# Third layer of a hyperbolic convolution: the sum over tokens as eight accumulated matmuls and a mask

## The chip, the cores and the metric

The kernel runs on one core of a Trainium2 chip. The metric is the device time of one execution in microseconds (us), as the median of several runs. TensorE (PE), VectorE (DVE), ScalarE (ACT) and GpSimd (POOL) run side by side and meet at semaphores; SyncE (SP) issues most transfers. All data are float32.

## The reference, cut to what matters

Eight stages work on x, which has 8 x 32 x 32 tokens of 64 channels, and each adds its result to x: a cosine transform, an expert layer, a dense convolution, an expert layer, the hyperbolic convolution that is changed here, an expert layer, a spherical transform, an expert layer. The hyperbolic one has three layers, each a fully connected map in the ball followed by a batch norm in the ball. The batch norm begins with a midpoint over all tokens:

```python
def midpoint(x):
    lx = lam(x)                       # 2 / (1 - |x|^2), one number for a token
    m = jnp.sum(lx * x, 0) / jnp.clip(jnp.sum(lx - 1.0, 0), TINY)
    n = jnp.sqrt(jnp.clip(jnp.sum(m * m), TINY))
    m = jnp.tanh(0.5 * jnp.arctanh(jnp.minimum(SC * n, ATANH_CLIP))) * m / (SC * n)
    return project(m)

def hbatchnorm(x, bias_pt, weight):
    mu = midpoint(flat)
    var = jnp.mean(dist(flat, mu) ** 2)
    v = logmap(mu, flat)
    v = transp(mu, bias_pt, v)
    v = jnp.sqrt(weight / (var + BN_EPS)) * v
    return expmap(bias_pt, v).reshape(shp)
...
out = hrelu(hbatchnorm(hconv(x, z1, 1, 1, 0, 64), bn1_bias, bn1_weight))
out = hrelu(hbatchnorm(hconv(out, z2, 3, 1, 1, 16), bn2_bias, bn2_weight))
out = hbatchnorm(hconv(out, z3, 1, 1, 0, 16), bn3_bias, bn3_weight)
out = hrelu(project(mobius_add(out, x)))
```

What matters is the numerator of the midpoint: a sum over all 8192 tokens of a number for the token times its row of channels, and, next to it, the sum of lam - 1 and every token's product with the bias.

## The kernel before

**Tiling.** The 8192 tokens lie on 128 partitions and in 64 tiles: X[p, t, c] holds channel c of token (p, t). A number for each token is a [128, 64] array (k.scalars), the values of the first two layers are V16 with 16 channels, those of the third V64 with 64, so that one DVE instruction on the third layer's values has 4096 elements on each partition. W1 and W2 are work arrays of the same shape.

**Stages.** `program` runs the eight stages one after the other; each is a block of its own with a barrier of all engines behind it. `hyper_stage` is the fifth.

**Order inside the stage.** The function `hyper` is written once and run by DVE, ACT and PE, each of which issues only its own steps. `Turns.step` counts the steps of each engine and lets an engine wait for a given count of another; `Ball.dve` makes every DVE step wait for the DVE step before it too. So DVE's order is the order of the text, and what is late there is late for all behind it. PE and ACT wait only for what a step names.

**The batch norm** (`batchnorm`, lines 2420 and following) gets V and, for each token, s and y2 = |x|^2, where V times s is the point. Lines 2432 to 2436 make lam = 2/(1 - y2) and dx = lam s. Then, up to the changed place: w1 = V dx, a product of 4096 elements (line 2437, recorded under the helper's line 2293); the sum of w1 over the tiles into cols[:, 0:c] by a reduction whose inner step runs over t, so with a stride of c elements (line 2438, helper 2304); lam - 1 and its sum into cols[:, c]; a matmul with a matrix of ones, which adds the c + 1 columns over the partitions and leaves the totals on every partition (line 2441); w1 = V bias and its sum over channels, bY; bY times s; and a copy of the totals out of PSUM. The step behind them, n = max(cols[:, c], TINY), is the first that is the same in both kernels. The helpers `tt`, `ts`, `stt`, `sum`, `rec` and `act` have one line each, so the trace gives the helper's line for nearly all of these steps.

**The head of the stage.** SP issues seven loads, first z1 alone (first_loaded), then six more (loaded). POOL sets four arrays (zeroed): ones, one, shifted_sum and shifted. Every engine waits at line 2686, for all four on ACT, for the first two on DVE and PE, and then for z1. DVE waits for the six other loads only behind its first pass over X.

**PE in the third layer.** `third` turns V16 (line 2929) and multiplies with z3 (line 2937), eight matmuls with 512 moving columns each; after that PE has only the small sums of lines 2441 and 2493 to do up to the end of the stage. The convolution of the second layer (lines 2886 to 2893) has matmuls with whole 128 x 128 stationaries (line 2886) and with cut ones of 32 x 16 and 16 x 32 (lines 2890 and 2892).

Of the kernel before, what the change touches and what calls it, by code (L numbers as in the profile page):

```python
# [15 lines left out]
P = 128  # L16
# [2266 lines left out]
class Ball:  # L2283
# [136 lines left out]
    def batchnorm(self, V, s, y2, bn, w1, w2, n_out, pieces):  # L2420
# [16 lines left out]
        self.tt(w1, V, self.over_c(dx, c), S)  # L2437
        self.sum(cols[:, 0:c], w1.rearrange("p t c -> p c t"))
        self.ts(lam, lam, -1.0, A)
        added = self.sum(cols[:, c:c + 1], lam)  # L2440
        total = self.pe(lambda: self.nc.tensor.matmul(k.sum_ps[:, 0:c + 1], k.ones[:, :], cols, start=True, stop=True),
                        added)
        self.tt(w1, V, self.over_t(bias), S)
        self.sum(bY, w1)
        self.tt(bY, bY, s, S)
        self.ts(cols, k.sum_ps[:, 0:c + 1], 1.0, S, need=[total])
# [97 lines left out]

    def relu(self, V, factor, n, root, rec_root, w1, rooted, made, pieces):
# [25 lines left out]
def hyper_stage(nc, sem, k):  # L2571
# [8 lines left out]
    with ExitStack() as ctx:  # L2580
        def sb(n, shape, dt=F32):
            return ctx.enter_context(nc.sbuf_tensor(f"hyp_{n}", shape, dt))
# [23 lines left out]
        eights = sb("eights", [P, OCTS, P])  # L2606
        k.sum_ps, sums_ps = psum("sum_ps", [P, 512]), psum("sums_ps", [P, 512])
        turn_ps = [psum(f"turn_ps{j}", [P, 512]) for j in range(2)]
        work_ps = [psum(f"work_ps{j}", [P, 512]) for j in range(2)]
        small_ps = [psum(f"small_ps{j}", [P, 512]) for j in range(2)]  # L2610
        first_loaded, loaded, zeroed = sem("hyp_first_loaded"), sem("hyp_loaded"), sem("hyp_zeroed")
# [6 lines left out]
        @block.sync  # L2618
        def _(sp):
            sp.dma_start(z1[:, :], dram["hyp_z1"]).then_inc(first_loaded, 16)  # L2620
            sp.dma_start(z2[:, :, :], dram["hyp_z2"]).then_inc(loaded, 16)
            sp.dma_start(z3[:, :, :], dram["hyp_z3"]).then_inc(loaded, 16)
            sp.dma_start(bias[:, :, :], dram["hyp_bias"]).then_inc(loaded, 16)
            sp.dma_start(weight[:, :], dram["hyp_weight"]).then_inc(loaded, 16)
            sp.dma_start(band[:, :, :], dram["hyp_band"]).then_inc(loaded, 16)
            sp.dma_start(side_by_side[:, :], dram["hyp_side_by_side"]).then_inc(loaded, 16)

        @block.gpsimd
        def _(pool):
# [3 lines left out]
            nc.gpsimd.memset(shifted[:, :, :, :], 0.0).then_inc(zeroed, 1)  # L2633

        LOADS = 6 * 16
# [4 lines left out]
        def hyper(me, eng):  # L2640
# [45 lines left out]
            eng.wait_ge(zeroed, 4 if me == "scalar" else 2)  # L2686
# [336 lines left out]
def shape_constants():  # L3023
# [11 lines left out]
    c["dc_one_row"][CH, :] = 1.0  # L3035
    rows = np.arange(TILES)
# [131 lines left out]
```

## Time and profile before

| | us |
|---|---|
| median of 3 runs | 2379.16 |
| lowest and highest | 2371.57 and 2380.84 |
| the profiled execution | 2385.53 |
| its span in the profile | 2383.7 |
| of it the hyperbolic stage | about 832 to 1206 |

The page of a profile gives the busy time of each engine over the span; the timeline gives single instructions with the time at which each starts, how long it takes and, in brackets, how long its engine stood idle before it and what released it; the windows view gives the busy time in a chosen stretch with the clock that PE was granted there, where 1.00 is 2.4 GHz and 0.50 is 1.2 GHz. PE's rows name the stationary as rows * columns and then the moving data.

### The profile page before, as it was taken

What the parts mean: (1) busy time and instruction counts of PE and PEld (TensorE: products, weight loads), DVE (VectorE), ACT (ScalarE), POOL (GpSimd) and SP (SyncE); (2) the same over time, 40 slices, a digit from 0 to 9 for tenths busy, and PEclk for the clock granted to TensorE, in tenths of its full rate; (3) what the DMA queues carried; (4) which work ended last, traced back from release to release, by engine and by line L of the source; (5) the groups of instructions that cost most, each with busy time, mean ns of one, the idle gap of its engine ahead of it and who ended that gap; (6) DMA issues with size and microseconds to landing.
All of it is one profiled execution on the core that took longest, in us unless ns stands there. A gap on an engine that the chain in (4) does not pass through costs nothing. (4 is left out here: it accounts for less than half of the span.)

```text
span 2383.7 us, 31881 instructions
## 1 busy us (share of the span) xinstructions
PE 1733.0 (73%) x11703; PEld 1018.0 (43%) x11703; DVE 1303.7 (55%) x2417; ACT 997.7 (42%) x1783; POOL 618.7 (26%) x617
## 2 busy tenths in 40 slices
PE   2899996879999942010024999999666449999995
PEld 2533333335333331000013666666455426666663
DVE  6543336665433366789984545555561755455554
ACT  2465653334665532361132444444233324444442
POOL 0100000001000000000025777433351357773332
PEclk8799997997999955555555999999877569999997
DMA  1222210011222100000012444444365125444453
GB/s 47 64 66 62 71 45 19 0 28 53 66 63 64 45 10 0 0 0 0 0 35 77 149 141 142 140 132 151 114 118 117 41 95 147 136 148 133 135 154 128
DMA packets 125738, 186.93 MB, mean 78 GB/s; under 512 B 39184, under 2 KB 73232, under 8 KB 125072
## 3 DMA queue, kind: packets, MB, share of 16 engines
q1 hardware_dynamic: 107408, 165.99, 24.1%
q0 software_dynamic: 18176, 18.91, 2.4%
q8 instruction: 93, 1.52, 0.3%
q14 instruction: 61, 0.50, 0.1%
HBM read 157.18 MB, written 27.65 MB: 78 GB/s over the span
## 5 line engine op out<-in xcount | busy, mean ns | idle before, releaser
L1333 DVE TENSOR_TENSOR ffn_hidden<-ffn_silu,ffn_up_ps 114x512 f32<-114x512 f32 x468 | 321.7, 687 | 398.1 <-ACT ffn_silu L1303 398.1
L1245 PE MATMUL ffn_up_ps<-ffn_turned,ffn_weights 64*114 64x256 f32 x3744 | 491.7, 395 | 21.1 <-DMA ffn_weights<-in_ffn_weights 13.8
L1303 ACT ACTIVATE ffn_silu<-ffn_up_ps 114x512 f32<-114x512 f32 x468 | 279.4, 597 | 445.6 <-PE ffn_up_ps L1245 443.8
L821 POOL DMA_INDIRECT slots<-ffn_rows,ffn_slot x256 | 253.4, 990 | 564.5 <-DVE ffn_slot L938 397.8
L736 ACT ACTIVATE ffn_hidden<-ffn_up_ps,ffn_b 128x512 f32<-128x512 f32 x512 | 309.4, 689 | 197.1 <-PE ffn_up_ps L631 197.0
L1224 POOL DMA_INDIRECT results<-ffn_yout,ffn_xin x312 | 300.3, 962 | 306.6 <-DVE ffn_yout L1321 237.4
L1245 PEld LDWEIGHTS ffn_up_ps<-ffn_turned,ffn_weights 64*114 64x114 f32 x3744 | 318.1, 176 | 136.4 <-issue 80.7
L631 PE MATMUL ffn_up_ps<-ffn_T,ffn_up_w 64*128 64x512 f32 x1024 | 260.8, 622 | 2.9 <-ACT ffn_hidden L736 2.9
L652 PE MATMUL ffn_y_ps<-ffn_hidden,ffn_down 128*64 128x512 f32 x1024 | 247.7, 605 | 3.7 <-DVE ffn_y_total L526 2.0
L1256 PE MATMUL ffn_y_ps<-ffn_hidden,ffn_weights 114*64 114x256 f32 x1872 | 236.4, 388 | 0.0
L526 DVE SCALAR_TENSOR_TENSOR ffn_gated<-ffn_y_ps,ffn_b,ffn_gates 128x512 f32<-128x512 f32 x96 | 72.0, 750 | 204.8 <-PE ffn_y_ps L652 203.2
L631 PEld LDWEIGHTS ffn_up_ps<-ffn_T,ffn_up_w 64*128 64x128 f32 x1024 | 91.1, 188 | 169.1 <-ACT ffn_hidden L736 93.3
L1256 PEld LDWEIGHTS ffn_y_ps<-ffn_hidden,ffn_weights 114*64 114x64 f32 x1872 | 120.5, 136 | 98.8 <-DVE ffn_hidden L1333 52.7
L652 PEld LDWEIGHTS ffn_y_ps<-ffn_hidden,ffn_down 128*64 128x64 f32 x1024 | 62.2, 136 | 161.6 <-ACT ffn_hidden L736 85.5
L1033 PE MATMUL ffn_turn_ps<-ident,D 128*128 128x128 f32 x64 | 17.2, 430 | 117.3 <-DVE D L874 117.3
L1234 PE MATMUL ffn_x_ps<-ident,ffn_xin 128*64 128x128 f32 x312 | 64.7, 290 | 34.3 <-DMA ffn_xin<-slots 34.3
L1267 PE MATMUL ffn_out_ps<-fold,ffn_y_half 128*128 128x64 f32 x624 | 87.9, 264 | 1.4 <-DVE ffn_y_half L1314 1.4
L526 DVE SCALAR_TENSOR_TENSOR ffn_y_total<-ffn_y_ps,ffn_b,ffn_gates 128x512 f32<-128x512 f32 x32 | 23.7, 750 | 112.8 <-PE ffn_y_ps L652 92.0
L1267 PEld LDWEIGHTS ffn_out_ps<-fold,ffn_y_half 128*128 128x128 f32 x624 | 82.4, 192 | 3.2 <-DVE ffn_y_half L1314 1.7
L1314 DVE COPY ffn_y_half<-ffn_y_ps 128x256 f32<-128x256 f32 x156 | 66.2, 424 | 20.0
L2630 POOL MEMSET hyp_ones<- 128x128 f32 x1 | 0.2, 205 | 288.6 <-POOLq L3000 288.6
L1948 POOL MEMSET dc_first<- 128x128 f32 x1 | 0.2, 204 | 288.3 <-POOLq L3000 288.3
(376 smaller groups left out, 2139.9 us busy)
## 6 DMA issues: line engine op xcount, KB each, us to landing
ffn_weights<-in_ffn_weights SPq DMA_DIRECT2D x156, 534.0 KB
ffn_gates<-gate_rows SPq DMA_DIRECT2D x128, 256.0 KB
ffn_xin<-slots SPq DMA_DIRECT2D x156, 66.0 KB
sht_mix<-in_sht_weights SPq DMA_DIRECT2D x8, 1024.0 KB, 8.2
results<-ffn_yout,ffn_xin POOLq DMA_INDIRECT x312
slots<-ffn_rows,ffn_slot POOLq DMA_INDIRECT x256, 2.2
D<-results SPq DMA_DIRECT2D x12, 256.0 KB, 4.7
ffn_second<-results SPq DMA_DIRECT2D x12, 256.0 KB, 6.0
```

The lines of the kernel that those rows point to most:

```text
L526: nc.vector.scalar_tensor_tensor(target, y_ps[th][:, :], b2[:, p:p + 1], gates[:, n % GATES, th, :], ALU.add, ALU.mult).then_inc(y_gated, 1)
L631: nc.tensor.matmul(up_ps[j][:, :], up_w[rows, 2 * p + half, c * P:(c + 1) * P], T[rows, g * NTOK:(g + 1) * NTOK], start=True, stop=True).t ...
L652: last = nc.tensor.matmul(y_ps[th][rows, :], down[:, 2 * p + half, c, :], hidden[:, n % 2 * UNITS + 2 * half + th, :], start=(c == 0), sto ...
L736: nc.scalar.activation(hidden[:, n % 2 * UNITS + j, :], up_ps[j][:, :], ACT.Gelu, bias=b1[:, bias_at:bias_at + 1], scale=1.0).then_inc(hid ...
L821: nc.gpsimd.indirect_dma_start(k.slots, bass.IndirectOffsetOnAxis(slot[c][:, t:t + 1], 0), rows[c][:, t, :], None).then_inc(row_stored[h], 16)
L1224: nc.gpsimd.indirect_dma_start(k.results, bass.IndirectOffsetOnAxis(xin[:, b % HELD, j, CH + 1:CH + 2].bitcast(I32), 0), yout[:, b % HELD, ...
L1245: last = nc.tensor.matmul(up_ps[w][n % 2][0:SIZE, chunk % 2 * BLOCK:(chunk % 2 + 1) * BLOCK], weights[rows_of, b % WEIGHTS, chunk * SIZE:( ...
L1256: last = nc.tensor.matmul(y_ps[b % 2][half * CH:(half + 1) * CH, 0:BLOCK], weights[0:SIZE, b % WEIGHTS, col:col + CH], hidden[0:SIZE, b % ...
L1267: last = nc.tensor.matmul(out_ps[:, j * CH:(j + 1) * CH], y_half[:, b % 2, j * P:(j + 1) * P], k.fold[:, :], start=True, stop=True)
L1303: nc.scalar.activation(silu[0:SIZE, n % 2, :], up_ps[0][n % 2][0:SIZE, :], ACT.Silu).then_inc(silu_done, 1)
L1314: nc.vector.tensor_copy(y_half[:, b % 2, :], y_ps[b % 2][:, 0:BLOCK]).then_inc(y_kept, 1)
L1333: nc.vector.tensor_tensor(hidden[0:SIZE, b % 2, c, :], silu[0:SIZE, n % 2, :], up_ps[1][n % 2][0:SIZE, :], ALU.mult).then_inc(hidden_done, 1)
```

## The change

It concerns the third layer alone (c == CH), in a new function `midpoint_sums`. PE makes the weighted sum over tokens: for each group of eight tiles the eight columns of dx are the stationary (128 x 8) and the group's V, 8 tiles of 64 channels, is the moving data (512 columns); the eight groups are accumulated in one PSUM bank, `across`. Its row i and block j hold the sum for tile i's weight and tile j's values, so only the blocks on the diagonal are wanted: DVE multiplies the eight rows with a mask of ones and zeros (`blocks`, loaded from DRAM) into `spread`. A second matmul with ones adds the eight rows over the partitions into the bank `beside`, and DVE adds the eight blocks there into cols[:, 0:64]. The sum of lam - 1 keeps its path through a small matmul. The product with the bias and its sum are issued between the group sums and the masked product. In the first two layers the copy of the totals now stands ahead of the product of bY with s.

At the head of the stage two memsets are added on POOL (coefs, 320 elements wide, which nothing reads, and spread, 512), DVE and ACT both wait for all six memsets, and SP issues an eighth load, the mask.

```diff
-        self.tt(w1, V, self.over_c(dx, c), S)
-        self.sum(cols[:, 0:c], w1.rearrange("p t c -> p c t"))
-        self.ts(lam, lam, -1.0, A)
-        added = self.sum(cols[:, c:c + 1], lam)
-        total = self.pe(lambda: self.nc.tensor.matmul(k.sum_ps[:, 0:c + 1], k.ones[:, :], cols, start=True, stop=True),
-                        added)
-        self.tt(w1, V, self.over_t(bias), S)
-        self.sum(bY, w1)
+        if c == CH:
+            self.midpoint_sums(V, dx, lam, bias, bY, cols, w1)
+        else:
...
+            self.sum(bY, w1)
+            self.ts(cols, k.sum_ps[:, 0:c + 1], 1.0, S, need=[total])
         self.tt(bY, bY, s, S)
-        self.ts(cols, k.sum_ps[:, 0:c + 1], 1.0, S, need=[total])
...
+    def midpoint_sums(self, V, weight, lam, bias, bY, cols, w1):
+        k, c = self.k, CH
+        across, beside = k.banks[0], k.banks[1]
+
+        def issue():
+            for g in range(8):
+                last = self.nc.tensor.matmul(across[0:8, :], weight[:, 8 * g:8 * g + 8],
+                                             V[:, 8 * g:8 * g + 8, :].rearrange("p t c -> p (t c)"),
+                                             start=(g == 0), stop=(g == 7))
+            return last
+        summed = self.pe(issue, self.t.at("vector"))
+        self.ts(lam, lam, -1.0, ALU.add)
+        added = self.sum(cols[:, c:c + 1], lam)
+        self.tt(w1, V, self.over_t(bias), ALU.mult)
+        self.sum(bY, w1)
+        masked = self.tt(k.spread[0:8, :, :], across[0:8, :].rearrange("p (t c) -> p t c", c=c), k.blocks[0:8, :, :],
+                         ALU.mult, summed)
+
+        def issue():
+            self.nc.tensor.matmul(k.sum_ps[:, 0:1], k.ones[:, :], cols[:, c:c + 1], start=True, stop=True)
+            return self.nc.tensor.matmul(beside[:, :], k.ones[0:8, :], k.spread[0:8, :, :].rearrange("p t c -> p (t c)"),
+                                         start=True, stop=True)
+        total = self.pe(issue, masked, added)
+        self.sum(cols[:, 0:c], beside[:, :].rearrange("p (t c) -> p c t", c=c), total)
+        self.ts(cols[:, c:c + 1], k.sum_ps[:, 0:1], 1.0, ALU.mult)
...
+            sp.dma_start(k.blocks[:, :, :], dram["hyp_blocks"]).then_inc(loaded, 16)
...
+            nc.gpsimd.memset(k.coefs[:, :, :], 0.0).then_inc(zeroed, 1)
+            nc.gpsimd.memset(k.spread[:, :, :], 0.0).then_inc(zeroed, 1)
+
+        LOADS = 7 * 16
...
-            eng.wait_ge(zeroed, 4 if me == "scalar" else 2)
+            eng.wait_ge(zeroed, 6 if me in ("scalar", "vector") else 2)
```

## Rows read from the trace of the kernel before

**Rows 1.** Section 1 of the page: each engine's busy time, share of the span, instructions.

```profile
PE 1733.0 (73%) x11703; PEld 1018.0 (43%) x11703; DVE 1303.7 (55%) x2417; ACT 997.7 (42%) x1783; POOL 618.7 (26%) x617
```

**Rows 2.** Windows view: stretch, length, busy time and instructions by engine, PE's clock, DMA.

```profile
831.80:1203.50 371.70, 57.37 (x208) 39.55 (x208) 294.72 (x552) 116.54 (x156) 1.33 (x4) 0.53 0.01 2
```

**Rows 3.** Timeline of the replaced steps, DVE and PE: start, length, instruction.

```profile
1079.34 4.42 DVE L2293 TENSOR_TENSOR hyp_W<-hyp_V,hyp_scalar 128x4096 f32<-128x4096 f32 x1
1083.80 6.98 DVE L2304 TENSOR_REDUCE hyp_cols<-hyp_W 128x64 f32<-128x4096 f32 x1
1090.81 0.20 DVE L2297 TENSOR_SCALAR hyp_scalar<-hyp_scalar 128x64 f32<-128x64 f32 x1
1091.04 0.22 DVE L2304 TENSOR_REDUCE hyp_cols<-hyp_scalar 128x1 f32<-128x64 f32 x1
1091.30 4.42 DVE L2293 TENSOR_TENSOR hyp_W<-hyp_V,hyp_bias 128x4096 f32<-128x4096 f32 x1
1091.32 0.69 PE L2441 MATMUL hyp_sum_ps<-hyp_cols,hyp_ones 128*128 128x65 f32 x2 [52.83 <-DVE hyp_cols L2304]
1095.76 4.42 DVE L2304 TENSOR_REDUCE hyp_scalar<-hyp_W 128x64 f32<-128x4096 f32 x1
1100.21 0.22 DVE L2293 TENSOR_TENSOR hyp_scalar<-hyp_scalar 128x64 f32<-128x64 f32 x1
1100.47 0.23 DVE L2297 TENSOR_SCALAR hyp_cols<-hyp_sum_ps 128x65 f32<-128x65 f32 x1
1100.73 0.15 DVE L2297 TENSOR_SCALAR hyp_one<-hyp_cols 128x1 f32<-128x1 f32 x1
```

**Rows 4.** Timeline of PE at both clocks; x is the count of records.

```profile
940.26 2.07 PE L2886 MATMUL hyp_small_ps<-hyp_shifted,hyp_band 128*128 128x512 f32 x2
942.27 0.82 PE L2890 MATMUL hyp_small_ps<-hyp_shifted,hyp_band 32*16 32x384 f32 x1
946.25 3.78 PE L2886 MATMUL hyp_small_ps<-hyp_shifted,hyp_band 128*128 128x512 f32 x4
1032.32 1.02 PE L2937 MATMUL hyp_small_ps<-hyp_z,hyp_eights 128*128 128x512 f32 x2
1033.18 1.88 PE L2937 MATMUL hyp_turn_ps<-hyp_z,hyp_eights 128*128 128x512 f32 x4
1782.62 3.29 PE L1786 MATMUL sht_spec_ps<-sht_forward_leg,sht_fourier 128*32 128x128 f32 x28 [2.98 <-issue]
```

**Rows 5.** Windows view of PE: stretch, length, busy (records), granted clock, DMA share, GB/s.

```profile
33.50:38.90 5.40, 5.40 (x25) 0.50 0.00 0
942.30:946.20 3.90, 3.90 (x13) 0.50 0.00 0
1028.80:1032.20 3.40, 3.40 (x10) 0.50 0.00 0
1032.30:1038.50 6.20, 6.19 (x15) 1.00 0.00 0
1782.70:1786.50 3.80, 3.80 (x51) 0.56 0.92 200
```

**Rows 6.** Groups of DVE by shape: count, busy us, mean ns, idle before.

```profile
L2293 DVE TENSOR_TENSOR hyp_V<-hyp_small_ps,hyp_scalar 128x512 f32<-128x512 f32 x2 | 1.4, 691 | 0.1
L2304 DVE TENSOR_REDUCE hyp_cols<-hyp_W 128x16 f32<-128x1024 f32 x2 | 3.7, 1859 | 0.1
```

**Rows 7.** Timeline at the stage's head, and DVE's first use of the other loads.

```profile
832.14 1.00 POOL L2633 MEMSET hyp_shifted<- 128x1088 f32 x1
833.45 0.23 ACT L2310 ACTIVATE hyp_sq<-hyp_z 128x32 f32<-128x32 f32 x1 [10.54 <-DMA hyp_z<-in_hyp_z]
833.46 1.22 DVE L2304 TENSOR_REDUCE hyp_mean<-X 128x16 f32<-128x1024 f32 x1 [2.50 <-DMA hyp_z<-in_hyp_z]
858.32 0.74 DVE L2293 TENSOR_TENSOR hyp_bias_sq<-hyp_bias 128x64 f32<-128x64 f32 x3
```

**Rows 8.** Weight loads of line 2892: shortest, median and longest in ns.

```profile
L2892 PEld LDWEIGHTS hyp_small_ps<-hyp_shifted,hyp_band x12: 101/114/173, 942.3 to 952.6; 16*32 16x32 f32 x12
```

More of the change, by code:

```diff
@@ L2436, in batchnorm @@
         self.tt(dx, lam, s, S)
-        self.tt(w1, V, self.over_c(dx, c), S)
-        self.sum(cols[:, 0:c], w1.rearrange("p t c -> p c t"))
-        self.ts(lam, lam, -1.0, A)
-        added = self.sum(cols[:, c:c + 1], lam)
-        total = self.pe(lambda: self.nc.tensor.matmul(k.sum_ps[:, 0:c + 1], k.ones[:, :], cols, start=True, stop=True),
-                        added)
-        self.tt(w1, V, self.over_t(bias), S)
-        self.sum(bY, w1)
+        if c == CH:
+            self.midpoint_sums(V, dx, lam, bias, bY, cols, w1)
+        else:
+            self.tt(w1, V, self.over_c(dx, c), S)
+            self.sum(cols[:, 0:c], w1.rearrange("p t c -> p c t"))
+            self.ts(lam, lam, -1.0, A)
+            added = self.sum(cols[:, c:c + 1], lam)
+            total = self.pe(lambda: self.nc.tensor.matmul(k.sum_ps[:, 0:c + 1], k.ones[:, :], cols, start=True,
+                                                          stop=True), added)
+            self.tt(w1, V, self.over_t(bias), S)
+            self.sum(bY, w1)
+            self.ts(cols, k.sum_ps[:, 0:c + 1], 1.0, S, need=[total])
         self.tt(bY, bY, s, S)
-        self.ts(cols, k.sum_ps[:, 0:c + 1], 1.0, S, need=[total])
         self.ts(n, cols[:, c:c + 1], TINY, ALU.max)
@@ L2543, in batchnorm @@
         return rooted, made
+    def midpoint_sums(self, V, weight, lam, bias, bY, cols, w1):
[9 more added lines that the diff above has]
+        self.ts(lam, lam, -1.0, ALU.add)
+        added = self.sum(cols[:, c:c + 1], lam)
+        self.tt(w1, V, self.over_t(bias), ALU.mult)
[9 more added lines that the diff above has]
+        self.ts(cols[:, c:c + 1], k.sum_ps[:, 0:1], 1.0, ALU.mult)
     def relu(self, V, factor, n, root, rec_root, w1, rooted, made, pieces):
@@ L2606, in hyper_stage @@
         eights = sb("eights", [P, OCTS, P])
+        k.blocks, k.spread = sb("blocks", [40, EIGHT, CH]), sb("spread", [40, EIGHT, CH])
+        k.coefs, k.coefs_t = sb("coefs", [P, OCTS, 40]), sb("coefs_t", [40, OCTS, P])
         k.sum_ps, sums_ps = psum("sum_ps", [P, 512]), psum("sums_ps", [P, 512])
@@ L2610, in hyper_stage @@
         small_ps = [psum(f"small_ps{j}", [P, 512]) for j in range(2)]
+        k.banks = [*turn_ps, *work_ps, *small_ps]
         first_loaded, loaded, zeroed = sem("hyp_first_loaded"), sem("hyp_loaded"), sem("hyp_zeroed")
@@ L2633, in _ @@
             nc.gpsimd.memset(shifted[:, :, :, :], 0.0).then_inc(zeroed, 1)
-        LOADS = 6 * 16
+            nc.gpsimd.memset(k.coefs[:, :, :], 0.0).then_inc(zeroed, 1)
+            nc.gpsimd.memset(k.spread[:, :, :], 0.0).then_inc(zeroed, 1)
+        LOADS = 7 * 16
         def flat(t):
@@ L3035, in shape_constants @@
     c["dc_one_row"][CH, :] = 1.0
+    c["hyp_blocks"] = np.zeros((40, 8, CH), np.float32)
+    for tile in range(8):
+        c["hyp_blocks"][tile, tile, :] = c["hyp_blocks"][32 + tile, tile, :] = 1.0
     rows = np.arange(TILES)
```

## The prediction

> **What bounds the kernel now.** First the busy shares of the page [rows 1]: PE is busy 73% of the span and DVE 55%, which says nothing yet on the place that is changed. The hyperbolic stage stands in one stretch of the windows view, 831.80 to 1203.50 us [rows 2]: of its 371.70 us DVE works 294.72, PE 57.37 and ACT 116.54. DVE is the engine to look at there, and every DVE step waits for the DVE step ahead of it, so what is taken from DVE while no other engine is late comes off the span one for one: the stages run one after the other with a barrier between them. Then the timeline of the steps that are replaced [rows 3]. From 1079.34 to 1100.73 DVE goes from one instruction to the next with gaps of 0.03 to 0.04 us and waits for nobody; PE does one small matmul in it, at 1091.32, whose result DVE takes up at 1100.47, long after. The chain there is DVE alone: product with dx 4.42, strided sum over tokens 6.98, the two steps on lam 0.20 and 0.22, product with the bias 4.42, its sum 4.42, bY 0.22, the copy of the column sums 0.23. With the gaps that is 1100.73 - 1079.34 = 21.39 us.
>
> **What leaves DVE.** The product with dx (start to start 1083.80 - 1079.34 = 4.46), the strided sum (1090.81 - 1083.80 = 7.01) and the 65-wide copy (1100.73 - 1100.47 = 0.26): 11.73 us. What stays of the 21.39 is 9.66: lam 0.23, its sum 0.26, bias product 4.46, sum 4.45, bY 0.26 [rows 3].
>
> **What runs beside it: the eight group sums on PE.** They need dx, ready when DVE's next step starts less its gap, at 1079.31; PE starts about 0.06 later, as it did after the column sum (DVE end 1091.26, PE start 1091.32), so at 1079.38 [rows 3]. The four DVE steps under which they lie end at 1079.34 + 0.23 + 0.26 + 4.46 + 4.45 = 1088.74. A float32 matmul shows as two records, one per pass (the two matmuls that line 2886 issues in a row from 946.25 leave four), so eight matmuls with 512 moving columns are 16 passes. At the lower clock two such passes took 2.07 and four 3.78: (3.78 - 2.07)/2 = 0.855 from start to start, and 1.22 for a last one with its tail. At the higher clock two took 1.02 and four 1.88: 0.43, and 0.59 for a last one [rows 4]. So:
> - all at the lower level: 15 x 0.855 + 1.22 = 14.0 us, end at 1093.4, 4.65 us after DVE wants it;
> - with the clock rising after T us: T/0.855 passes at the low rate, the rest at 0.43, plus 0.16 for the last one's tail. A burst that began at 1028.76 was at 1.00 from 1032.2 on (T = 3.4), and a busy stretch from 33.50 to 38.90 was still at 0.50 at its end (T of at least 5.4, taken as 5.5) [rows 5]. This gives 8.7 us for 3.4, 9.3 for 4.5 and 9.8 for 5.5, so ends at 1088.1, 1088.6 and 1089.2: a stall of 0 to 0.5 us. I take T = 4.5, the middle, and no stall.
>
> Which of the two it is decides the case. PE has been idle for 52.83 us ahead of 1091.32 [rows 3], so the sums begin at granted 0.50, which is 1.2 GHz. For a rise: unbroken work with 128 rows is what the rise at 1032.2 follows, and the stretch from 1782.70, whose stationaries have 128 rows and only 32 columns, has a mean of 0.56, so the rise falls into it [rows 4, 5]. Against it: from 942.30 to 946.20 PE was busy without a gap and stayed at 0.50, with stationaries of 32 rows by 16 columns, and 16 by 32 among them [rows 4, 5]. The new stationaries have 128 rows and 8 columns, a shape that this trace lacks. By its rows it resembles the first sort, by its columns the second. I lean to the rise, since the 32-column work did raise the clock.
>
> The Trainium skill ("TensorE: Matmul & The Clock Gate", Part 1: The HAM clock gate) has it that the throttled state is the default and that PE activity releases it, with no word on how wide the stationary must be. By that rule alone the sums finish in time; the row from 942.30 shows a busy engine that was not released, so the lower level keeps a chance of its own.
>
> **What is added on DVE's path behind the sums.** The masked product reads 8 x 512 out of PSUM: products of 512 columns out of PSUM take 0.69 [rows 6], and fewer partitions don't shorten it in any row, 0.73 with the gap. Then PE: the one-column matmul with ones and the wide one with ones[0:8] and 512 columns. At the higher clock: two passes with 512 columns 1.02 [rows 4], and before them two loads of 128 columns with one-column passes, 0.58 at the lower level by the 65-wide pair less its width, some 0.4 at the higher; 1.4 in all. At the lower level: 0.5 for the small one, and 2.07 [rows 4] for the wide one, 2.6. Handing over to PE and back: 2 x 0.06. Then the sum over eight groups, 512 elements out of PSUM with a stride of 64 elements. No row shows it. Below, 512 elements without a stride, 0.69 [rows 6]; above, the strided sum of 1024 elements takes 1.86, half of which and a half start cost is 0.93 to 1.0 [rows 6]. I take 1.0, since stride is what that row shares, and 1.04 with the gap. Last the one-wide copy out of PSUM, 0.19 with gap (the 1-wide step at 1100.73 takes 0.15).
> - Rise: masked product from 1088.74, PE from 1089.50 to 1090.90, sum from 1090.95, copy 1091.99, bY 1092.18, and the next step (n) at 1092.44 where it was at 1100.73: **8.3 us gained** (7.8 with the 0.5 stall, 8.6 with the short sum).
> - Lower level: masked product from 1093.45, PE from 1094.2 to 1096.8, sum from 1096.85, copy 1097.9, n at 1098.35: 2.4 us gained.
>
> **What is added elsewhere.** Two memsets on POOL, 320 and 512 elements wide, and both DVE and ACT now wait for all six at the head of the stage. The last memset of now is 1088 wide and takes 1.00 [rows 7]. Its share of 832/1088 is 0.77 us; with a start cost for each of the two, some 0.9 (0.77 to 1.0). It ends at 833.14, so the sixth ends at 834.04. DVE and ACT started at 833.46 and 833.45, both released by the load of z [rows 7]. Everything of the stage hangs on these two, so **0.6 us is lost** (0.45 to 0.7), on the path and with no cover. The eighth load, the mask (80 KB), is queued behind the other seven on SP and nothing waits behind it; it is awaited before the squares of the bias at 858.32 [rows 7], over 20 us after the stage's first work: nothing, unless it took that long. The swap of copy and bY in layers one and two costs nothing: PE's small matmul (0.69) has a product and a sum of a quarter of 4.42 each ahead of the copy, 2.2 us of cover [rows 3]. PE reading V beside DVE reading V: the product at 1091.30, with PE at work under its head, took the same 4.42 as the one at 1079.34 without [rows 3]; nothing, and were the 8.9 us of DVE work slowed by 1%, 0.1.
>
> **Sum.** 8.3 - 0.6 = 7.7 us off the span of 2383.7. The profiled run took 2385.53, which is 1.8 beyond its span, and would take 2377.8. It lies 0.27% above the median of the three runs, 2379.16, from which I count: 2379.16 - 7.7 = **2371.5**.
>
> **Rivals.**
> - *The clock stays at 0.50.* 2.4 - 0.6 = 1.8 us gained: 2377.4. For it the row from 942.30, against it the one from 1782.70.
> - *Exposed weight loads, on top of the lower clock (the other side).* In [rows 4] loads hide under passes. If an 8-column load does not hide, each of the 16 passes grows. A 32-column load takes 0.10 to 0.17 [rows 8]; 16 x 0.16 = 2.6 us against a gain of 1.8: 0.8 slower, 2380.0. The point from which it decides is 1.8/16 = 0.11 us a pass; with the 0.34 that a 128-column load can take it is 3.6 slower, 2382.8. Against it: loads of 128 columns hid between the passes of [rows 4], where these are 8 wide.
> - *The gain is given back later.* PE's following bursts meet the clock's rise at other moments once they begin 8 us sooner; T ran from 3.4 to 5.5, and a us more at the low level costs half a us. The stages behind have some eight such bursts; were all a whole us later, 4 us go: 2375.5. Nothing says that they would all go one way.
>
> For the first of these, the same skill page (section LDWEIGHTS) says that a load's time goes with its columns; by it an 8-column load is too short to matter, which the 32-column row supports.
>
> **Chances.** Rise 0.60 (2371.5), lower clock 0.28 (2377.4), exposed loads 0.05 (2380.0), given back 0.07 (2375.5). Three runs of before spread over 9.3 us, so each case is some 4 us wide either way. Two in ten are left out between 2366 and 2380.5. A measurement can tell about 0.5% from no change, 11.9 us; DVE gives up only 11.73 us in all, so a gain beyond that needs the spread of the medians: faster 0.11, same 0.86, slower 0.03.
>
> **What would show it.** In the profile after: the group sums as 16 records with 128*8 stationaries from some 0.06 after dx, 9.3 us long with the granted clock rising under them (or 14 with 0.50 throughout); DVE's masked product directly behind the sum of bY (or idle 4.7 before it, released by PE); one DVE idle of 1.5 (or 2.7) under the wide matmul; the short sum at 0.7 to 1.0; from dx's end to n 13.1 us (or 19.0) where it was 21.4; the first DVE and ACT step of the stage 0.6 later, released by POOL. The prediction is wrong if passes are longer than 0.855, or if the strided sum out of PSUM takes well over 1.0.

## The result and the profile after

| | before | after |
|---|---|---|
| median of 20 runs each, taken in turns, us | 2381.43 | 2374.3 |
| lowest and highest | 2364.96 and 2384.02 | 2367.68 and 2379.26 |
| profiled execution and its span | 2385.53 and 2383.7 | 2368.77 and 2366.6 |
| mean granted PE clock | 0.835 | 0.842 |

The ratio is 0.9974, with a 95% interval from 0.9964 to 0.9984. On 2381 us that is **6.2 us faster, 3.8 to 8.6** (the two medians of the table differ by 7.1, which lies inside the interval). The gain is within the 0.5% that the prediction counted as no change. It had summed up a gain of 7.7. In absolute time the kernel came out 2.8 us above its 2371.5, most of it because the kernel before had a median of 2381.43 over these 20 runs where the prediction counted from 2379.16.

**The changed piece.** The timeline of the kernel after, from the step that makes dx; each row has start, length, engine, line, operation, tiles and, in brackets, the idle time ahead of it and what ended it. [rows 3] is the same piece before.

```profile
1071.69 0.23 DVE L2293 TENSOR_TENSOR hyp_scalar<-hyp_scalar 128x64 f32<-128x64 f32 x1
1071.95 0.19 DVE L2297 TENSOR_SCALAR hyp_scalar<-hyp_scalar 128x64 f32<-128x64 f32 x1
1071.97 9.74 PE L2557 MATMUL hyp_turn_ps<-hyp_V,hyp_scalar 128*8 128x512 f32 x16 [40.86 <-DVE hyp_scalar L2293]
1072.17 0.22 DVE L2304 TENSOR_REDUCE hyp_cols<-hyp_scalar 128x1 f32<-128x64 f32 x1
1072.43 4.42 DVE L2293 TENSOR_TENSOR hyp_W<-hyp_V,hyp_bias 128x4096 f32<-128x4096 f32 x1
1072.78 0.14 PEld L2557 LDWEIGHTS hyp_turn_ps<-hyp_V,hyp_scalar 128*8 128x8 f32 x1 [0.72 <-issue]
...
1076.89 4.42 DVE L2304 TENSOR_REDUCE hyp_scalar<-hyp_W 128x64 f32<-128x4096 f32 x1
...
1079.40 0.09 PEld L2557 LDWEIGHTS hyp_turn_ps<-hyp_V,hyp_scalar 128*8 128x8 f32 x1 [0.34 <-issue]
...
1081.81 0.68 DVE L2293 TENSOR_TENSOR hyp_spread<-hyp_turn_ps,hyp_blocks 8x512 f32<-8x512 f32 x1 [0.50 <-PE hyp_turn_ps L2557]
...
1082.54 0.38 PE L2570 MATMUL hyp_sum_ps<-hyp_cols,hyp_ones 128*128 128x1 f32 x2 [0.84 <-DVE hyp_spread L2293]
...
1082.86 1.12 PE L2571 MATMUL hyp_turn_ps<-hyp_spread,hyp_ones 8*128 8x512 f32 x2
1084.08 0.69 DVE L2304 TENSOR_REDUCE hyp_cols<-hyp_turn_ps 128x64 f32<-128x512 f32 x1 [1.59 <-PE hyp_turn_ps L2571]
1084.81 0.16 DVE L2297 TENSOR_SCALAR hyp_cols<-hyp_sum_ps 128x1 f32<-128x1 f32 x1
1085.00 0.23 DVE L2293 TENSOR_TENSOR hyp_scalar<-hyp_scalar 128x64 f32<-128x64 f32 x1
1085.26 0.15 DVE L2297 TENSOR_SCALAR hyp_one<-hyp_cols 128x1 f32<-128x1 f32 x1
```

Read down DVE's rows: the product with dx and the long strided sum are gone, and the two steps of 4.42 us stand directly behind dx. PE's 16 passes over the same V run beside them, and both steps take 4.42 all the same, as in [rows 3]. DVE then waits 0.50 for PE, does the masked product, waits 1.59 for the wide matmul, and sums in 0.69. "The piece" below is the time from the first DVE step after dx to the step that makes n: 1085.26 - 1071.95 = 13.31 us, where [rows 3] give 21.39. That is 8.08 less.

**PE's clock under the group sums**, windows view of the kernel after, PE alone: window, length, busy time and records, granted clock (0.50 is 1.2 GHz, 1.00 is 2.4 GHz), DMA.

```profile
1072.00:1077.40 5.40, 5.40 (x7) 0.50 0.00 0
1077.60:1081.70 4.10, 4.10 (x10) 1.00 0.00 0
```

The clock rose 5.4 to 5.6 us after the sums began. The spacing of the loads says the same: idle 0.72 between them at first, 0.34 at the end.

**The head of the stage**, timeline of the kernel after, against [rows 7]:

```profile
822.85 0.20 POOL L2666 MEMSET hyp_ones<- 128x128 f32 x1 [288.64 <-POOLq L3038]
...
824.12 0.36 POOL L2670 MEMSET hyp_coefs<- 128x320 f32 x1
...
824.43 0.52 POOL L2671 MEMSET hyp_spread<- 40x512 f32 x1
...
824.99 1.22 DVE L2304 TENSOR_REDUCE hyp_mean<-X 128x16 f32<-128x1024 f32 x1 [2.99 <-POOL hyp_spread L2671]
...
826.47 0.93 SPq L2662 DMA_DIRECT2D hyp_blocks<-in_hyp_blocks  x1
```

DVE's first step comes 824.99 - 822.85 = 2.14 us after the first memset. Before, the first memset was at 831.82 and DVE began at 833.46 [rows 7], 1.64 us later, released by the load of z. So 0.50 is lost. The mask's load is the last thing on SP's queue, and the profile shows no engine waiting for it.

**The stage as a whole**, windows view of the kernel after; the columns are those of [rows 2], and the window runs from the first memset to about the same work as there:

```profile
822.85:1188.25 365.40, 68.89 (x226) 41.74 (x226) 284.71 (x552) 116.55 (x156) 2.10 (x6) 0.54 0.01 2
```

DVE has 10.0 us less work than in [rows 2] (284.71 for 294.72), PE has 11.5 more (68.89 for 57.37, in 18 more records), POOL 0.8 more.

**Where the rest of the profile's 17.1 us is.** The two profiled spans differ by 17.1 us (2383.7 and 2366.6), far more than the medians do. Cut at the first DVE step of each stage, the stages are, in us (each is the difference of two start times in the trace, the last one runs to the end of the span):

| execution | cosine transform | experts 1 | dense convolution | experts 2 | **hyperbolic** | experts 3 | spherical transform | experts 4 |
|---|---|---|---|---|---|---|---|---|
| before | 42.8 | 314.5 | 156.8 | 309.8 | **373.6** | 522.5 | 125.4 | 528.7 |
| before, again | 41.7 | 311.4 | 156.9 | 309.6 | **369.7** | 522.1 | 120.4 | 528.1 |
| after | 42.8 | 305.9 | 156.1 | 310.5 | **366.8** | 520.8 | 125.2 | 528.9 |
| after, again | 42.2 | 314.8 | 156.1 | 310.6 | **366.7** | 521.0 | 125.1 | 529.4 |

8.6 us of the 17.1 are in the first expert stage, which the change does not touch. The windows view of PE over it, first the kernel before:

```profile
64.00:73.60 9.60, 9.60 (x47) 0.50 0.02 6
73.90:93.50 19.60, 19.60 (x90) 0.50 0.00 1
94.00:104.00 10.00, 9.23 (x37) 1.00 0.16 53
```

and the kernel after:

```profile
64.00:73.60 9.60, 9.60 (x46) 0.50 0.03 11
73.90:93.50 19.60, 18.35 (x119) 1.00 0.02 7
```

The same instructions met the clock's rise near 73.7 us in one execution and near 93.6 in the other. At half the clock for 19.6 us, some 9.8 us of work at 2.4 GHz is left undone, about the 8.6 that the stage differs by. So one profile beside another says nothing on a gain of 6 us unless it is cut down to the piece.

### The profile page after: what moved, and what is told of

The parts are those of the page before. It is cut to its first block and busy times, and to the rows that moved or that the text cites. A ratio compares the mean times of both kernels' runs of the same rounds, so it can differ in the third digit from the quotient of the medians.

```text
span 2366.6 us, 31921 instructions
## 1 busy us (share of the span) xinstructions
PE 1735.5 (73%) x11721; PEld 1013.4 (43%) x11721; DVE 1294.2 (55%) x2417; ACT 997.9 (42%) x1783; POOL 619.5 (26%) x619
## 5 line engine op out<-in xcount | busy, mean ns | idle before, releaser
L736 ACT ACTIVATE ffn_hidden<-ffn_up_ps,ffn_b 128x512 f32<-128x512 f32 x512 | 309.6, 688 | 198.0 <-PE ffn_up_ps L631 197.9
L2123 PE MATMUL dc_conv_ps<-dc_fresh,dc_step_w 128*128 128x512 f32 x144 | 67.6, 617 | 8.8 <-DVE dc_fresh L2109 8.8
```

The costliest lines, as they stand in the source:

```text
L736: nc.scalar.activation(hidden[:, n % 2 * UNITS + j, :], up_ps[j][:, :], ACT.Gelu, bias=b1[:, bias_at:bias_at + 1], scale=1.0).then_inc(hid ...
```

## The experiments

All ratios are to the kernel before, run on the same chip among the runs of the kernel, with a 95% interval; a ratio is turned into us on 2381. In the expectations the piece is written as the time from dx to n.

**1. The piece without the work (cut_sum).** The kernel before, with the product and the strided sum of the third layer replaced by a copy of one tile's columns.

```diff
-        self.tt(w1, V, self.over_c(dx, c), S)
-        self.sum(cols[:, 0:c], w1.rearrange("p t c -> p c t"))
+        if c == CH:
+            self.ts(cols[:, 0:c], V[:, 0, :], 1.0, S)
+        else:
+            self.tt(w1, V, self.over_c(dx, c), S)
+            self.sum(cols[:, 0:c], w1.rearrange("p t c -> p c t"))
```

> The kernel before, with the third layer's product with dx and its strided sum over tokens left out (cols gets the first tile's values instead, one 64-wide step), so the midpoint's numerator is not computed. Theory A (what DVE gives up there comes off the span one for one): 11.47 us of DVE go and 0.22 come, so 11.2 us off, a ratio near 0.9953; in the profile the steps from dx to n take 10.1 us where they took 21.4. Theory B (a part of the gain is given back in later bursts of PE): the same 10.1 us in the profile, but only 6 to 8 us off the time, and the stages behind longer by the rest.

Measured: 2371.28, ratio 0.9962 (0.9947 to 0.9977), so -9.0 us (-12.6 to -5.5). Timeline:

```profile
1069.84 0.20 DVE L2297 TENSOR_SCALAR hyp_cols<-hyp_V 128x64 f32<-128x64 f32 x1
...
1070.55 4.43 DVE L2293 TENSOR_TENSOR hyp_W<-hyp_V,hyp_bias 128x4096 f32<-128x4096 f32 x1
...
1079.98 0.15 DVE L2297 TENSOR_SCALAR hyp_one<-hyp_cols 128x1 f32<-128x1 f32 x1
```

The piece is 10.14 us, 11.25 shorter than [rows 3]: what is taken from DVE there leaves the piece one for one, and this is about the most that a change of this sum alone can bring in this order of steps. The change got 8.08 of it.

**2. The head (no_head, head_only).** The change without the two memsets and with the old waits; and the kernel before with the memsets, the mask's load and the new waits alone.

```diff
-            nc.gpsimd.memset(k.coefs[:, :, :], 0.0).then_inc(zeroed, 1)
-            nc.gpsimd.memset(k.spread[:, :, :], 0.0).then_inc(zeroed, 1)
-            eng.wait_ge(zeroed, 6 if me in ("scalar", "vector") else 2)
+            eng.wait_ge(zeroed, 4 if me == "scalar" else 2)
```

> The changed kernel without the two memsets (coefs is read by nothing, and of spread only the rows that the masked product writes are read), with the waits at the stage's head as they were: four on ACT, two on DVE and PE. Theory A (the sixth memset released DVE and ACT, 0.49 us later than the load of z): first DVE step again about 1.65 us after the first memset, where it was 2.14, released by the load; 0.5 us off, not to be told apart in the time from the changed kernel: ratio to before 0.997 as there. Theory B (the load of z lands late on its own): it stays at 2.1.

> The kernel before with the head of the change alone: the two memsets, the mask load and the waits for all six memsets on DVE and ACT. Theory A (the head costs 0.5 us and nothing else of it reaches the path): the first DVE step 2.14 us after the first memset instead of 1.64, the stage else as before, ratio 1.0002. Theory B (an edit that moves so little can still shift the time by some us, because unchanged stages take their clock's rises at other moments): the stages outside the changed one differ between the profiles by more than the stage does, and the ratio may be off 1.0002 by 0.001.

Measured: no_head 2374.69, 0.9974 (0.9963 to 0.9985); head_only 2381.43, 0.9997 (0.9981 to 1.0013). The times can't tell 0.5 us apart, but the timelines can. In no_head the first memset is at 832.13 and DVE begins 1.83 us later, released by the load again:

```profile
833.96 1.22 DVE L2304 TENSOR_REDUCE hyp_mean<-X 128x16 f32<-128x1024 f32 x1 [2.70 <-DMA hyp_z<-in_hyp_z]
```

In head_only the first memset is at 831.80 and DVE begins 2.14 us later, released by POOL:

```profile
833.94 1.22 DVE L2304 TENSOR_REDUCE hyp_mean<-X 128x16 f32<-128x1024 f32 x1 [2.99 <-POOL hyp_spread L2638]
```

So the head costs 0.3 us against no_head, where the load of z landed later than in the kernel before, and 0.5 us against the kernel before. In none of these profiles does an engine wait for the mask's load.

**3. The cover (serial).** The change with the product and sum of the bias moved from under the group sums to behind the short sum.

```diff
         added = self.sum(cols[:, c:c + 1], lam)
-        self.tt(w1, V, self.over_t(bias), ALU.mult)
-        self.sum(bY, w1)
...
         self.ts(cols[:, c:c + 1], k.sum_ps[:, 0:1], 1.0, ALU.mult)
+        self.tt(w1, V, self.over_t(bias), ALU.mult)
+        self.sum(bY, w1)
```

> The changed kernel with the product with the bias and its sum issued behind the short sum instead of ahead of the masked product, so that PE's group sums have only 0.5 us of DVE work over them. Theory A (the change gains because 9.4 us of DVE work hide the group sums): DVE idles 9.3 us before the masked product, dx to n takes 13.3 + 8.9 = 22.2 us, and the kernel is about 1 us slower than before, ratio 1.0005. Theory B (the gain comes from cheaper work and not from the overlap): about as the changed kernel, ratio 0.997.

Measured: 2385.5, ratio 1.0016 (1.0001 to 1.0031), +3.8 us (0.2 to 7.4). Timeline:

```profile
1079.57 8.91 PE L2557 MATMUL hyp_turn_ps<-hyp_V,hyp_scalar 128*8 128x512 f32 x16 [40.87 <-DVE hyp_scalar L2293]
...
1088.59 0.68 DVE L2293 TENSOR_TENSOR hyp_spread<-hyp_turn_ps,hyp_blocks 8x512 f32<-8x512 f32 x1 [8.59 <-PE hyp_turn_ps L2557]
...
1100.95 0.15 DVE L2297 TENSOR_SCALAR hyp_one<-hyp_cols 128x1 f32<-128x1 f32 x1
```

DVE now stands idle for 8.59 us, and the piece is 1100.95 - 1079.55 = 21.40 us, to 0.01 that of before. TensorE makes this sum no sooner than DVE did: from dx to the bias product it is 1091.78 - 1079.55 = 12.23 us here, and 1091.30 - 1079.34 = 11.96 in [rows 3]. So by the piece the change gains because 9.4 us of other DVE work lie over the sum, and by nothing else. The piece came out 0.8 below the 22.2 expected, since the sums took 8.9 where the expectation had reckoned with the 9.7 of the first profile. The time is 3.3 us worse than the piece says; see the table below.

**4. What raises the clock (rows32).** The change with the group sums over 32 of the 128 partitions; the rest of the sum is left out. Columns, passes and time per pass are the same.

```diff
-                last = self.nc.tensor.matmul(across[0:8, :], weight[:, 8 * g:8 * g + 8],
-                                             V[:, 8 * g:8 * g + 8, :].rearrange("p t c -> p (t c)"),
+                last = self.nc.tensor.matmul(across[0:8, :], weight[0:32, 8 * g:8 * g + 8],
+                                             V[0:32, 8 * g:8 * g + 8, :].rearrange("p t c -> p (t c)"),
```

> The changed kernel with the group sums made over 32 of the 128 partitions only (stationaries of 32 rows by 8 columns, the same 16 passes of 512 columns), so three quarters of the tokens are left out of the midpoint's numerator. Theory A (the clock rose under the group sums because their stationaries have 128 rows, however few columns; the cut stationaries of the convolution left it at 0.50): the granted clock stays at 0.50, the sums take 14.0 us instead of 9.7, DVE idles 4.7 instead of 0.5, dx to n takes 13.3 + 4.2 + 1.1 = 18.6 us; ratio to before 0.999. Theory B (any unbroken work raises it): as the changed kernel, 9.7 us and 13.3 us.

Measured: 2382.82, ratio 1.0013 (1.0003 to 1.0024), +3.1 us (0.7 to 5.7). Timeline, then the windows view of PE:

```profile
1080.41 13.81 PE L2557 MATMUL hyp_turn_ps<-hyp_V,hyp_scalar 32*8 32x512 f32 x16 [40.86 <-DVE hyp_scalar L2293]
...
1094.33 0.68 DVE L2293 TENSOR_TENSOR hyp_spread<-hyp_turn_ps,hyp_blocks 8x512 f32<-8x512 f32 x1 [4.58 <-PE hyp_turn_ps L2557]
...
1095.59 2.07 PE L2571 MATMUL hyp_turn_ps<-hyp_spread,hyp_ones 8*128 8x512 f32 x2
...
1098.94 0.15 DVE L2297 TENSOR_SCALAR hyp_one<-hyp_cols 128x1 f32<-128x1 f32 x1
```

```profile
1080.50:1094.20 13.70, 13.70 (x16) 0.50 0.00 0
```

This is the prediction's rival of the lower clock, brought about by the edit. PE is busy for 13.7 us without a gap and is never granted more than 0.50; DVE waits 4.58 (4.65 was worked out); the wide matmul takes 2.07; the piece is 1098.94 - 1080.39 = 18.55 us, a gain of 2.84 in place of 8.08. The stationaries have 8 columns in both. With 128 rows the clock rose under the sums in all five profiles in which PE had stood idle for 40.9 us ahead of them: 5.4 or 5.5 us after their start in the change and in after_again, 3.8 or 3.9 us after it in serial, no_head and pick. With 32 rows it did not rise in 13.7 us. That is one profile, and experiment 7 shows a burst of mixed shapes that stayed at 0.50 nearly as long before the clock rose, so it is strong evidence but not proof. The time is 5.4 us worse than this piece says (2.84 less 0.5 for the head is a gain of 2.3); see the table below.

**5. The clock raised ahead (warm).** The change with seven unneeded matmuls of the same shape issued when V is ready, so that PE is not cold when the sums begin.

```diff
         each(lambda h, w: self.tt(v[h], a[h], v[h], ALU.mult, w))
+        if c == CH:
+            def busy():
+                for g in range(7):
+                    last = self.nc.tensor.matmul(self.k.banks[2][0:8, :], self.k.ones[:, 0:8],
+                                                 V[:, 0:8, :].rearrange("p t c -> p (t c)"), start=True, stop=True)
+                return last
+            self.pe(busy, self.t.at("vector"))
```

> The changed kernel with seven extra matmuls of PE (8-column stationaries of ones over V, 512 columns, results unused) issued when V is ready, so that PE is at work in the 9.9 us before dx. Theory A (the group sums take 9.7 us because 5.6 us of them run at the lower clock, and the 0.50 us idle of DVE comes from that): the group sums take 7.0 us at 1.00 throughout, DVE does not idle before the masked product, dx to n takes 12.8 us instead of 13.3. Theory B (DVE's idle has another cause): 13.3 stays. In the time both are within the error: ratio near 0.997.

Measured: 2374.61, 0.9973 (0.9959 to 0.9987). Timeline:

```profile
1068.77 7.87 PE L2406 MATMUL hyp_work_ps<-hyp_V,hyp_ones 128*8 128x512 f32 x14 [30.99 <-DVE hyp_V L2293]
...
1078.64 8.73 PE L2564 MATMUL hyp_turn_ps<-hyp_V,hyp_scalar 128*8 128x512 f32 x16 [2.01 <-DVE hyp_scalar L2293]
...
1088.02 0.68 DVE L2293 TENSOR_TENSOR hyp_spread<-hyp_turn_ps,hyp_blocks 8x512 f32<-8x512 f32 x1
```

DVE's wait is gone and the piece is 1091.47 - 1078.62 = 12.85 us, as expected. But the sums took 8.73 and not 7.0. The windows view of PE shows why:

```profile
1078.70:1082.00 3.30, 3.30 (x5) 0.55 0.00 0
1082.50:1087.30 4.80, 4.80 (x12) 1.00 0.00 0
```

The clock had risen under the unneeded matmuls (7.87 us for 14 passes, where all at 0.50 would be 12), and it fell again some 0.4 us after the sums began. The 9.4 us of cover hid that: once the sums end under the cover, a faster clock is worth nothing more to them.

**6. The step behind the sums (pick, pick_warm, pick_early).** The step behind the sums is what the cover doesn't hide: mask, wide matmul, short sum and the one-wide copy, 1085.00 - 1081.81 = 3.2 us in the change. pick has ACT copy the eight rows, then eight small matmuls, each with a stationary that has ones in one row, collect 64 columns; the short sum becomes a 64-wide copy. It has no memsets. pick_warm adds the matmuls of experiment 5. pick_early also moves the one-column matmul, its copy and the product of bY with s in front of that copy.

```diff
-        masked = self.tt(k.spread[0:8, :, :], across[0:8, :].rearrange("p (t c) -> p t c", c=c), k.blocks[0:8, :, :],
-                         ALU.mult, summed)
+        kept = self.act(k.spread[0:8, :, :].rearrange("p t c -> p (t c)"), across[0:8, :], ACT.Copy, summed)
...
-            return self.nc.tensor.matmul(beside[:, :], k.ones[0:8, :], k.spread[0:8, :, :].rearrange("p t c -> p (t c)"),
-                                         start=True, stop=True)
+            for i in range(8):
+                last = self.nc.tensor.matmul(beside[:, 0:c], k.pick[0:8, i, :], k.spread[0:8, i, :],
+                                             start=(i == 0), stop=(i == 7))
```

> The changed kernel without the head's memsets and waits, and with another way behind the group sums: ACT copies the eight rows out of PSUM, eight small matmuls (stationary 8 x 128 with one row of ones, 64 moving columns) take the diagonal blocks and add them, and DVE copies 64 columns; no masked product and no short sum on DVE. Theory A (the tail behind the sums is serial, so only its own length counts while PE is the late one): ACT 0.6, PE 2.3, DVE 0.2 in place of DVE 0.7, PE 1.5, DVE 0.7, so dx to n about 13.5 us, no gain over 13.3; minus the head's 0.5. Theory B (taking two steps off DVE gains them): dx to n 11.9 us.

> The two edits together: PE at work before dx, and the diagonal taken by ACT and PE. Theory A (with the sums done after 7.0 us, copy and small matmuls fall under the 9.4 us of DVE work): group sums end 7.0 us after dx, ACT 0.6, PE done at 10.1, DVE idles 0.8, dx to n 10.9 us instead of 13.3; with the head's 0.5 that is 2.9 us better than the changed kernel, ratio to before 0.9956. Theory B (extra work of PE ahead delays the group sums): their start is more than 0.1 us after dx and the gain shrinks by as much.

> The kernel with PE at work before dx and the diagonal taken by ACT and PE, with three steps moved into DVE's and PE's waits: the one-column matmul right behind the group sums, its copy and bY times s ahead of the 64-wide copy. Theory A (behind the sums only the chain ACT copy, small matmuls, 64-wide copy counts): dx to n 10.2 us instead of 10.9, ratio to before 0.9953, a better kernel than the changed one by 3.6 us. Theory B (DVE's own steps are the bound again): 10.9 stays.

Measured: pick 2369.57 over only 5 runs, 0.9951 (0.9933 to 0.9969); pick_warm 2372.32, 0.9959 (0.9944 to 0.9973); pick_early 2373.04, 0.9972 (0.9961 to 0.9982). Timeline of pick_warm:

```profile
1077.52 7.03 PE L2564 MATMUL hyp_turn_ps<-hyp_V,hyp_scalar 128*8 128x512 f32 x16 [1.88 <-DVE hyp_scalar L2293]
...
1084.59 0.59 ACT L2310 ACTIVATE hyp_spread<-hyp_turn_ps 8x512 f32<-8x512 f32 x1 [11.45 <-PE hyp_turn_ps L2564]
...
1085.61 1.99 PE L2578 MATMUL hyp_turn_ps<-hyp_spread,hyp_pick 8*128 8x64 f32 x16
1087.71 0.23 DVE L2297 TENSOR_SCALAR hyp_cols<-hyp_turn_ps 128x64 f32<-128x64 f32 x1 [0.85 <-PE hyp_turn_ps L2578]
...
1088.42 0.15 DVE L2297 TENSOR_SCALAR hyp_one<-hyp_cols 128x1 f32<-128x1 f32 x1
```

Here a PE that is already at 1.00 pays: the copy on ACT and the small matmuls can begin while DVE is still busy, so the 7.03 us of sums let DVE wait only 0.85. The pieces are 12.88 (pick), 10.92 (pick_warm) and 10.10 us (pick_early), where the change has 13.31 and 13.5, 10.9 and 10.2 were expected. In pick the sums took 8.99 us, not the 9.74 of the first profile, which is the miss of 0.6. The times order them otherwise: pick_early has the shortest piece and the least gain of the three. All three intervals overlap that of the change, so none of them is shown to be faster than it.

**7. The same kernels again (before_again, after_again).** No edit.

> The kernel before, with no edit. Theory A (the spans of two profiles differ by the first expert stage, whose clock rises either near 74 or near 94 to 100 us, and by a us or two in other stages, whatever the kernel): ratio 1.0000, hyperbolic stage within 1 us of the 373.6 of the first profile, the other stages as before but for such an early or late rise. Theory B (the differences outside the changed stage belong to the edit): all stages within 0.5 us of the first profile.

> The changed kernel, with no edit, beside the last version on one chip. Theory A (its gain is 8.1 us less 0.5, give or take the moment at which the clock rises under the group sums and in the matmuls ahead of them): dx to n between 12.8 and 13.4 us, first expert stage near 314 in this profile as in most, ratio 0.9968, within the error of 0.9974. Theory B (a part is given back behind the stage): the same 12.8 to 13.4, and the stages behind together over 1 us longer than before's.

Measured: before_again 1.0004 (0.9993 to 1.0016); after_again 2374.07, 0.9984 (0.9973 to 0.9996), -3.8 us (-6.4 to -1.0). Its piece was 13.29 us and DVE's wait 0.47, as in the first profile. The kernel before came out 1.0 us slower than itself, which is within the error. The 0.9968 expected of after_again lies outside its interval. The hyperbolic stage of before_again was 3.9 us shorter than that of before, where at most 1 was expected. The difference lies in the second layer's convolution, ahead of the piece: there the pair of wide matmuls that takes 2.07 in [rows 4] took

```profile
936.01 1.13 PE L2886 MATMUL hyp_small_ps<-hyp_shifted,hyp_band 128*128 128x512 f32 x2
```

because the clock had already risen. The whole burst of PE in the windows view, before and then before_again:

```profile
936.80:950.20 13.40, 13.40 (x34) 0.50 0.00 1
936.10:949.50 13.40, 11.33 (x45) 1.00 0.00 0
```

Before, PE was busy for 13.4 us without a gap and stayed at 0.50, with stationaries of 64 and 128 rows in the first 5.5 and the last 4 us of it; in before_again the same instructions ran at 1.00, those of 32 and 16 rows too. The clock rose 13.5 us after the burst began in one execution (936.74 to 950.3) and 3.5 us after it in the other (932.48 to 936.0), with one and the same kernel. The whole span of before_again was 14.2 us shorter than that of before, with the same instructions.

**The pieces against the times.** The second column is the piece, less the 21.39 us of before, plus 0.5 where the two memsets are in. All in us against before.

| kernel | by its piece | by its times (95%) |
|---|---|---|
| the change | -7.6 | -6.2 (-8.6 to -3.8) |
| after_again | -7.6 | -3.8 (-6.4 to -1.0) |
| no_head | -8.5 | -6.2 (-8.8 to -3.6) |
| warm | -8.0 | -6.4 (-9.8 to -3.1) |
| cut_sum | -11.2 | -9.0 (-12.6 to -5.5) |
| serial | +0.5 | +3.8 (0.2 to 7.4) |
| rows32 | -2.3 | +3.1 (0.7 to 5.7) |
| pick | -8.5 | -11.7 (-16.0 to -7.4) |
| pick_warm | -10.5 | -9.8 (-13.3 to -6.4) |
| pick_early | -11.3 | -6.7 (-9.3 to -4.3) |
| head_only | +0.5 | -0.7 (-4.5 to 3.1) |
| before_again | 0 | +1.0 (-1.7 to 3.8) |

Six kernels came out 1.4 to 3.8 us worse than their piece (the first six of the table), rows32 5.4 and pick_early 4.6 worse; pick_warm, head_only and before_again within 1.2; pick 3.2 better. Three intervals, those of after_again, rows32 and pick_early, do not contain what the piece says, so this is more than the intervals allow for.

Two things on record bear on it. First, **a part lies outside the profiled span.** The time of an execution is 1.7 to 1.9 us longer than its span in all 83 executions of the kernel before whose span was recorded and in all 53 of cut_sum, head_only, before_again and the three pick kernels. In the change it is 2.1 to 5.4 us longer, 2.7 in the mean of 20; in after_again, no_head, serial and rows32 the mean is 2.5 to 2.6, and in warm 2.1. So in these six kernels 0.3 to 0.8 us of the shortfall is not in any stage. Which of their instructions brings it is not shown: the mask's load and the memsets alone (head_only) do not. Second, **medians are not means here.** By the mean span, no_head is 8.1 us below the kernel before and cut_sum 11.4, near the 8.5 and 11.2 of their pieces. For the change, whose runs of the kernel before have no recorded span, the mean time of those less 1.85 is 2378.0, against a mean span of 2371.1: 6.9 us, where the piece says 7.6. But after_again is 5.1 below (7.6 by its piece), warm 5.6 (8.0) and pick_early 6.6 (11.3), and serial is 3.6 above (0.5) and rows32 1.8 above (2.3 below). This part stays open.

## Why the prediction was right, point by point

- **The bound.** That the steps replaced are a chain on DVE alone, worth their length: right. cut_sum took 11.47 us of steps out (4.46 and 7.01 in [rows 3]), put 0.23 in, and the piece fell by 11.25. In the time it was 9.0, with 11.2 inside the interval.
- **Rise or no rise of the clock.** It rose, as in the likeliest case, about 5.5 us after the start, the late end of the 3.4 to 5.5 that the rows gave, where 4.5 was taken. The sums took 9.74 us for 9.3, and DVE waited 0.50 for an expected 0. In serial, pick and no_head they took 8.9 to 9.0 us, so 9.74 is the late end of a spread, not a constant. The choice of the likeliest case, by the rows of the stationary and not by its columns, is what rows32 bears out at one pair of sizes and in one profile: at 32 rows the clock stayed at 0.50 for 13.7 us. By the rule of the Trainium skill ("TensorE: Matmul & The Clock Gate", Part 1: The HAM clock gate), that activity releases the throttle, rows32 should have risen too, if its busy 13.7 us count as activity; the trace disagrees, and the measurement decides.
- **The two rows behind that choice were weaker than they looked.** The mean of 0.56 from 1782.70 on [rows 5] was read as a rise inside that stretch. It is a fall: the clock was still up for the first 0.5 us, then at 0.50, and rose only behind the stretch, as the windows view of PE in the kernel before shows:

```profile
1782.70:1783.20 0.50, 0.50 (x8) 0.95 0.93 82
1783.30:1786.50 3.20, 3.20 (x46) 0.50 0.92 223
1786.70:1788.00 1.30, 1.26 (x80) 1.00 1.06 216
```

  A rise did follow on work with 32 columns, so the conclusion held, but by luck: the row that was cited for it shows a fall. And the 3.9 us at 0.50 from 942.30 on, cited against the rise, are shorter than the 5.4 us for which the change's own 128 rows stayed at 0.50, and part of the 13.4 us shown in experiment 7; by themselves they say nothing on rows.
- **The rival of the lower clock.** Its price was worked out as a gain of 2.4 in the piece; rows32 measured 2.84, and most of the difference is the 0.31 of the short sum.
- **Weight loads.** The 8-column loads took 0.09 to 0.14 us, and none lengthened a pass: 0.14 + 0.72 is the 0.86 of a pass, 0.09 + 0.34 the 0.43. The rival of exposed loads did not come to pass. That a load's time goes with its columns is not what the rows show at this end: 8 columns took 0.09 to 0.14 us, and 32 columns 0.10 to 0.17 [rows 8].
- **Masked product and the work behind it.** 0.73 expected and measured. PE from 1082.54 to 1083.98 is 1.44 for 1.4.
- **The short sum.** Taken as 1.0, measured 0.69, the lower bound. This term was mis-sized by 0.31: the row of the strided sum of 1024 elements was taken as the nearest because of its stride, and the 512-wide rows out of PSUM [rows 6] would have been the better choice. It nearly pays for the 0.50 of waiting: the piece of 13.31 lies so near the 13.1 forecast by the luck of two errors that cancel.
- **The head.** 0.6 expected, 0.50 measured, released by POOL as said. The two memsets took 0.36 and 0.52 with an overlap, 824.95 - 824.12 = 0.83 in all.
- **The sum.** Piece and head give 8.08 - 0.50 = 7.6 for 7.7. The times give 6.2, whose interval holds 7.6, and then 3.8 in the repeat, whose interval does not. Of the shortfall 0.6 to 0.8 us lie outside the span, by the mean of the executions. **What stays open** is where the rest of the 1 to 4 us is. The prediction's third rival, a gain given back by later stages, is not shown: the three stages behind the piece sum up to 1176.6 and 1170.6 us in the two profiles of before and 1174.9 and 1175.5 in those of after. Nor do all 13 profiles show it: from n to the end of the span it was 1277.0, 1282.7 and 1282.9 us in the three whose piece is that of before (before_again, head_only, before), 1280.9 in the mean, and 1277.2 to 1283.5 in the ten others, 1280.3 in the mean. It is not ruled out either, since a spread of 6 us is more than what is sought, and each profile is one execution. Within the hyperbolic stage, ahead of the piece, both profiles of the change have 0.3 to 0.4 us less in the second layer's convolution and 1.4 more in the matmuls of `third` (line 2937 before). The windows view of PE in the first of them, to be read against 1028.80:1032.20 and 1032.30:1038.50 in [rows 5]:

```profile
1020.00:1026.10 6.10, 6.10 (x13) 0.50 0.00 0
1026.30:1031.00 4.70, 4.70 (x12) 1.00 0.00 0
```

  There the clock rose 6.2 us after the burst began, where it was 3.4 before. pick_early has the same 1.4 us, before_again 0.8, head_only 1.1, and the seven others differ from before by 0.2 at most, so it is not shown to belong to the change; where it occurs, it takes a part of the gain. What is shown is that shifts of 3 to 9 us in a stage occur between two profiles of one kernel with no edit at all. Whether a change in the piece moves them one way on average could only be read from many profiles of each kernel, which weren't taken.

## What to carry to other kernels

Work moved from a busy engine to an idle one is worth what other work of the busy engine lies over it: here PE was no faster at the sum than DVE, and the whole gain of the piece came from the 9.4 us of cover. Look next at the steps behind the covered part, since these alone are still on the path. Where PE starts cold and the cover is only just long enough, work out its time at both clocks, and look in several profiles at how long bursts of the same shape stay at the lower one before counting on the rise. Read a mean clock between the two levels in shorter windows: it can be a fall as well as a rise.

## What was not expected of the hardware

- **The moment of the clock's rise changes the length of a whole stage.** One and the same first expert stage was at 0.50 until near 73.7 us in one execution and 93.6 in another, 305.9 and 314.5 us long; over all profiles that stage ran from 304.4 to 315.6, and two profiles of the unchanged kernel differ by 14.2 us in span, 0.6%. The Trainium skill (same page and part) says that the number of slow matmuls differs from run to run of one kernel, and puts the cost of the ramp under 1% of a span; both agree with this, but 0.6% is more than twice the effect under study.
- **The clock fell after one short pause and not after two others.** After a gap of 2.01 us in warm the clock was at 0.55 in the mean of the next 3.3 us; after gaps of 1.88 (pick_warm) and 1.18 us (pick_early) it stayed up, and the 16 passes took 7.03 both times. Each is one profile.
- **The stride costs nothing in the short sum.** Summing 512 elements out of PSUM with a stride of 64 took 0.69 us, the time of an unstrided product of that size [rows 6], while 4096 out of SBUF with that stride took 6.98 against 4.42 [rows 3].
